# First weights split in the third stage, down weights asked for ahead of the next unit's operands, stores in pieces, low parts of sums apart

## The reference

```python
x = x + 0.5 * quantised_linear(layernorm(x))      # 6-bit weights, unpacked: (w - zero_point) * scale, plus bias
x = x + s4_convolution(layernorm(x))              # causal, 512 long, kernel from a state space model
x = x + 0.5 * quantised_linear(layernorm(x))
x = x + 0.5 * gated_ffn(layernorm(x))             # (silu(x Wg^T) * (x Wu^T)) Wd^T, F = 1376
x = x + s4_convolution(layernorm(x))              # the second state space model
x = x + 0.5 * gated_ffn(layernorm(x))
```

## Time and profile before

| | |
|---|---|
| median of 3 runs | 897.93 us (897.38 to 899.24) |
| profiled execution: its own time | 898.32 us |
| its span, first to last instruction | 896.5 us |
| mean granted TensorE clock | 0.994 |
| PE busy | 880.9 us (98%) |
| DVE busy | 621.2 us (69%) |
| ACT busy | 313.7 us (35%) |
| POOL busy | 372.2 us (42%) |

### The profile page before, as it was taken

How to read it: one execution, slowest core, us unless ns; L and a number is a source line. 1 busy time by engine, 2 the same in 40 slices (tenths; PEclk the granted TensorE clock), 3 DMA queues, 4 the chain that set the end, 5 groups by cost and what they waited for, 6 DMA issues and landing times.

```text
span 896.5 us, 11735 instructions
## 1 busy us (share of the span) xinstructions
PE 880.9 (98%) x4116; PEld 722.2 (81%) x4116; DVE 621.2 (69%) x1058; ACT 313.7 (35%) x517; POOL 372.2 (42%) x728
## 2 busy tenths in 40 slices
PE   8999999999999999999999999999999999999998
PEld 4878887788888877888888878888888788888876
DVE  7989778899999786555566877555667865454553
ACT  4534456534444351222323532222234511122211
POOL 6768567444444343332334452322334532222211
PEclk7999999999999999999999999999999999999999
DMA  8200000166677775564555655464646667556455
GB/s 326 105 1 1 1 1 2 72 240 244 251 272 280 246 232 176 163 183 151 168 163 153 200 165 188 134 189 125 206 142 212 184 179 244 171 180 208 129 158 171
DMA packets 41358, 148.27 MB, mean 165 GB/s; under 512 B 3538, under 2 KB 3794, under 8 KB 39892
## 3 DMA queue, kind: packets, MB, share of 16 engines
q0 software_dynamic: 29040, 100.93, 37.0%
q1 hardware_dynamic: 12260, 46.59, 13.5%
HBM read 117.36 MB, written 30.15 MB: 165 GB/s over the span
## 4 chain that ended last, share of the span: by engine, by line
PE 83%; DVE 6%; POOL 4%; DMA 3%; issue 3%; ACT 2%; SPq 0%; POOLq 0%; ACTq 0%; DVEq 0%
PE front L1469 15%; PE front L1471 15%; PE front L1470 15%; PE acc L1423 8%; PE acc L1425 7%; PE acc L1424 7%; PE front L480 3%; PE acc L1351 3%; PE acc L1350 3%; PE acc L1349 3%; DMA down_weights<-saved_down 2%; DVE hidden_lo L1250 2%; PE front L1351 1%; PE front L1350 1%; PE front L1349 1%
## 5 line engine op out<-in xcount | busy, mean ns | idle before, releaser
L1469 PE MATMUL front<-row_operands_hi,weight_operands 128*128 128x512 f32 x616 | 242.3, 393 | 1.6 <-DVE weight_operands L615 1.5
L1471 PE MATMUL front<-row_operands_hi,weight_operands 128*128 128x512 f32 x616 | 239.9, 390 | 0.0
L1470 PE MATMUL front<-row_operands_lo,weight_operands 128*128 128x512 f32 x616 | 239.9, 389 | 0.0
L1210 DVE TENSOR_TENSOR snapshots<-front,snapshots 128x512 f32<-128x512 f32 x132 | 91.0, 689 | 78.8 <-PE front L1471 77.5
L1423 PE MATMUL acc<-down_weights,hidden_hi 128*128 128x512 f32 x352 | 140.1, 398 | 5.2 <-DMA down_weights<-saved_down 3.4
L1469 PEld LDWEIGHTS front<-row_operands_hi,weight_operands 128*128 128x128 f32 x616 | 115.7, 188 | 28.0 <-issue 2.9
L1425 PE MATMUL acc<-down_weights,hidden_lo 128*128 128x512 f32 x352 | 137.4, 390 | 0.0
L1424 PE MATMUL acc<-down_weights,hidden_hi 128*128 128x512 f32 x352 | 137.2, 390 | 0.0
L1471 PEld LDWEIGHTS front<-row_operands_hi,weight_operands 128*128 128x128 f32 x616 | 115.6, 188 | 24.3
L1470 PEld LDWEIGHTS front<-row_operands_lo,weight_operands 128*128 128x128 f32 x616 | 115.7, 188 | 23.3
L831 POOL DMA_DIRECT2D weight_operands<-saved_weights x66 | 48.6, 736 | 188.4 <-PE front L1471 173.2
(11 more groups left out here) (177 smaller groups left out, 1352.4 us busy)
## 6 DMA issues: line engine op xcount, KB each, us to landing
weight_operands<-saved_weights POOLq DMA_DIRECT2D x33, 1280.0 KB, 6.3
down_weights<-saved_down POOLq DMA_DIRECT2D x77, 512.0 KB, 4.2
saved_weights<-weight_operands SPq DMA_DIRECT2D x11, 1792.0 KB, 6.7
weight_operands<-saved_weights POOLq DMA_DIRECT2D x33, 512.0 KB, 4.2
raw_weights<-wgu SPq DMA_DIRECT2D x11, 512.0 KB, 3.4
saved_down<-down_weights SPq DMA_DIRECT2D x11, 512.0 KB, 3.3
x_rows<-x_in SPq DMA_DIRECT2D x3, 1024.0 KB, 12.1
raw_down<-wdown SPq DMA_DIRECT2D x11, 256.0 KB, 2.9
```

Of the source, the lines that this page charges most:

```text
L1210: V.tensor_tensor(out, sum_of(k, product)[:], other, ALU.add).then_inc(front_read, 1)
L1469: T.matmul(o, wh, xh, start=(j == 0), stop=False)
L1470: T.matmul(o, wh, xl, start=False, stop=False)
L1471: last = T.matmul(o, wl, xh, start=False, stop=(j == 1))
```

## The change

It has four parts; the arithmetic is the same.

1. The split of the weights of step 0 moves from the last items before the units (items 50 to 53) to items 28 to 31 (`WEIGHTS_AT` = 28), on ACT, DVE and POOL.
2. In the last step of a unit POOL asks for the down weights of pass 1 of the turn (`load_down(q + 2)`) before the first operands of the next unit's step 1, and not after them. The wait for the end of the pass now stands ahead of both.
3. The 1024 KB store of the first half is cut into four of 256 KB, each after a further odd pass of the turn (1, 3, 5, 7).
4. In the turns of units 0 to 2, at `j` = 1 to 8, POOL made two low parts after asking for the down weights. Now it waits for the pass, makes one low part, asks for the down weights, and makes the other.

```diff
--- before.py
+++ after.py
@@ -30,6 +30,8 @@
 LN_SLOTS = 8
 
 SECOND_AT = TILES + 2
+
+WEIGHTS_AT = SECOND_AT + 10
 XT_SLOTS = 4
 EMB_SLOTS = 2
 
@@ -701,10 +703,12 @@
                     if u == 3 and f in (2, 4, 6, 8):
                         store(2, 1, f // 2 - 1, f // 2)
                 if u >= 2:
-                    store(u, 0, 0, BLK)
+                    for r in range(BLK):
+                        wait_pass(sp, PASSES * u + FT + 2 * r + 1)
+                        store(u, 0, r, r + 1)
             for r in range(BLK):
                 store(3, 1, r, r + 1)
-            sp.wait_ge(stored, 16 * (2 + 2 * BLK))
+            sp.wait_ge(stored, 16 * 4 * BLK)
 
 
         @block.gpsimd
@@ -815,7 +819,7 @@
                 for later, which in ((3, (0, 1)), (2, (2, 3))):
                     if n + later < PRE and second_of_pair(n + later):
                         sums_lo_step(pool, ITEMS[n + later].number // 2, which)
-                if n == PRE - 3:
+                if n == WEIGHTS_AT + 3:
                     down_weight_lo(pool, 0)
 
             def load_split(k, operands, product, arrived):
@@ -861,9 +865,12 @@
                         rstd_step(pool, n)
                     if q + 1 < FT:
                         down_weight_lo(pool, q + 1)
+
+                    if q + 2 >= FT and f == FT - 1:
+                        load_down(q + 2)
                     if k + 2 >= FT:
                         load_split(k + 2, FIRST_OPERANDS, M7, w_first_in)
-                    if q + 2 >= FT:
+                    if q + 2 >= FT and f < FT - 1:
                         load_down(q + 2)
                     if k + 2 >= FT:
                         load_split(k + 2, LAST_OPERANDS, M3, w_last_in)
@@ -875,9 +882,15 @@
                 for n in STATS_OF_STEP[u][FT - 1]:
                     rstd_step(pool, n)
                 for j in range(-1, FT - 1):
-                    load_down(PASSES * u + FT + j + WD_RING)
+
                     if u + 1 < UNITS and 1 <= j <= 2 * BLK:
-                        sums_lo_step(pool, BLK * (u + 1) + (j - 1) // 2, (0, 1) if j % 2 else (2, 3))
+                        pair, first = BLK * (u + 1) + (j - 1) // 2, 0 if j % 2 else 2
+                        wait_pass(pool, PASSES * u + FT + j)
+                        sums_lo_step(pool, pair, (first,))
+                        load_down(PASSES * u + FT + j + WD_RING)
+                        sums_lo_step(pool, pair, (first + 1,))
+                    else:
+                        load_down(PASSES * u + FT + j + WD_RING)
 
 
         @block.scalar
@@ -937,9 +950,9 @@
                     den_square()
                 if n in (13, SECOND_AT + 6):
                     toe_round(0 if n == 13 else 1)
-                if n == PRE - 6:
+                if n == WEIGHTS_AT:
                     weight_hi_raw(act, 0)
-                if n == PRE - 4:
+                if n == WEIGHTS_AT + 2:
                     weight_hi_sums(act, 0)
                     down_weight_hi(act, 0)
 
@@ -1196,11 +1209,11 @@
                     strip_lo(0 if n == 14 else 1)
                 if n in (13, SECOND_AT + 6):
                     strip(0 if n == 13 else 1)
-                if n == PRE - 6:
+                if n == WEIGHTS_AT:
                     weight_sums_a(dve, 0)
-                if n == PRE - 5:
+                if n == WEIGHTS_AT + 1:
                     weight_sums_b(dve, 0)
-                if n == PRE - 3:
+                if n == WEIGHTS_AT + 3:
                     weight_lows(dve, 0, (RAW, SUMS, FOURTH))
 
             def add(k, product, read, out, other):
```

## The result

The changed kernel takes 892.71 us, the median of 4 runs (891.92 to 893.25). The kernel before, beside it, takes 897.91 us (897.38 to 899.24). The ratio on record is 0.9935, with a 95% interval of 0.9923 to 0.9947. The profiled execution took 892.72 us, with a span of 890.9 us.

What follows compares the result with a forecast made beforehand. PE, busy 880.9 of 896.5 us, was taken as the bound, so only its waits count. Terms -1.0 - 1.0 + 0.35 - 1.4 - 0.4 - 1.1 = -4.6 us gave 893.3 us, range 891.8 to 896.3.

Steps and rivals of the forecast that it cites:

- What bounds the kernel: Whole span: PE is busy 880.9 of 896.5 us, so only its waits, 6.5 us at the places named, can be won.
- Part 1: Start of unit 0: PE's 1.48 us wait for the first low parts goes, less 0.5 of lateness: -1.0 us.
- the lateness of 0.5 us at the first pair: Third stage: DVE reaches the first pair's sums 0.2 to 1.3 us late, taken as 0.5, all passed on to PE.
- Part 2: Turns of units 0 and 1: -1.0 us (1.34 wait gone, new 0.3 before pass 2), then a loss of 0.35.
- Unit 2: Turn of unit 2: the 1.64 us wait before pass 2 shrinks to 0.2, a gain of 1.4 us.
- Part 3 in unit 3: Unit 3: loads beside a 256 KB piece land in 4.8 us, within about 5.0, so the 0.40 wait goes: -0.4 us.
- Part 4: Turns of units 0 to 2: six waits for `hidden_lo` go, 1.37 us, less 0.25 for later loads: -1.1 us.
- the 0.25 set aside for late loads: Turns of units 0 to 2: cost of down-weight loads issued 0.75 us later, set at 0.25 us in all (0 to 1.0).
- the third stage takes it back: Rival, chance 0.17: DVE 1.5 us late at the first pair, late loads eat half the `hidden_lo` gain; -3.1, 894.8 us.
- parts 2 and 3 don't do what they say: Rival, chance 0.11: queued transfers share engines, unit 0's wait stays, unit 1 gets 1.0, unit 2 keeps half; -2.35, 895.6 us.
- an issue stands behind DVE: Rival, chance 0.05: in the turns POOL's issue waits for DVE's `hidden_lo`, each load 0.4 us later; -2.2, 895.7 us.
- The slow series: Rival, chance 0.04: the four transfers at each turn land 13 us after first issue, not 10.1; +4.4, 902.3 us.

Runs made afterwards that it cites:

- run 8: The changed kernel with DVE's three low parts of the first weights one item later, behind the first pair's sums: 894.70 us, ratio 0.9961.
- run 3: The changed kernel with the operands again asked for before the down weights at every turn: 892.10 us, ratio 0.9912.
- run 12: The kernel before with only the first-half stores cut into 256 KB pieces, measured again for a profile: 896.72 us, ratio 0.9983.
- run 1: The kernel before with only the split of the first weights moved to earlier items: 897.21 us, ratio 0.9973.
- run 2: The kernel before with only POOL's two low parts set apart, the down-weight load between them: 896.24 us, ratio 0.9965.
- run 4: The changed kernel with one 1024 KB first-half store per unit again instead of four pieces: 899.48 us, ratio 1.0000.
- run 10: The changed kernel with down weights ahead of the operands in the turn of unit 0 alone, unit 3's store still in pieces: 892.81 us, ratio 0.9923.
- run 5: The changed kernel with down weights ahead in unit 0 alone and unit 3's first-half store as one transfer behind the ninth pass: 890.52 us, ratio 0.9907.
- run 6: The changed kernel with only unit 3's first-half store made one 1024 KB transfer behind the ninth pass: 892.84 us, ratio 0.9934.
- run 11: The changed kernel with down weights ahead in unit 0 alone and unit 3's store whole behind the ninth pass, measured again: 890.89 us, ratio 0.9916.
- run 9: The changed kernel as it is, measured again against the kernel before: 892.79 us, ratio 0.9933.

## Why the forecast was right, and where it was not

**What bounds the kernel**, and that only PE's waits can be won, holds: every microsecond of the gain lies at one of the places that the earlier trace rows led to.

**Part 1** was forecast at -1.0 and is -1.8. The step that failed is the lateness of 0.5 us at the first pair, with its lower end of 0.2: measured is 0. It took DVE's listed idle time, 1.92 us, as the whole cover, where 2.04 or a little more were there for 2.05 of work, and had POOL's bias meet the end of the low parts. POOL's operations were the ones to stand, its bias moved away, and the pair began on time. The other 0.3 us are the hidden price of the wait. That the chain has no cover for lateness is right (run 8).

**Part 2** in units 0 and 1 is right in place and sign, each within 0.25 us: no wait before pass 1, a new one of 0.35 before pass 2, a loss at unit 1. Terms of the same size with opposite signs cancel, so that the part is worth nothing beside the others (run 3).

**Unit 2** is right for the sum of parts 2 and 3 (-1.2 for -1.4). What the forecast did not price is what either would do alone. Part 3 alone brings -1.9 at this wait (run 12), more than the two together. Part 2 without it costs some 5 us: parts 1 and 4 alone gain 1.8 and 2.8 us (runs 1 and 2), and run 4, which has both and part 2, gains nothing.

**Part 3 in unit 3** has the wrong sign: +0.49 for -0.4. The step that failed is the landing of "4.2 + 0.6 = 4.8 us" for a load beside a piece. As a mean it is near: 22 such loads, in the six profiles with pieces in unit 3, land after 4.9 us. But they spread from 3.9 to 7.1, and one that takes more than the 5.1 to 5.2 us that are there is enough. In the profile of the change it takes 5.9. The wait of 0.40 did go, and a larger one came at 879 us. Waits of 0.19 to 1.56 us stand there in four of the six profiles (the change, runs 3, 10 and 12) and in none of the three in which the store comes late (runs 5, 6 and 11), whose loads take 3.6 to 4.0 us. In two more with pieces (runs 8 and 9) no load was slow enough. So the pieces make the wait possible, and chance decides each time whether it comes; why one load takes 4 and the next 6 us stays open.

**Part 4** has the right mechanism and is mis-sized: -3.15 for -1.1. The term that was mis-sized is what a removed wait is worth: the forecast took the listed 0.2 us, and some 0.5 came. Of the 2.0 missing, some 1.6 are the 0.27 us at each of six waits beyond their listed idle time; the rest is the 0.25 set aside for late loads, and rounding. That the profiled execution did not pay for late loads was luck: in six of ten profiles with part 4 they cost 0.35 to 1.2 us at the place near 336 us (run 9). The load was issued 0.5 us later than before, not 0.75.

**The sum** is 1.1 us short for the profiled executions (-4.6 for -5.7) and 0.6 us for the medians. It is so near since the two gains that were too small, 2.9 us together, stand against a start-up 0.39 later, 0.9 lost in unit 3 and 0.5 in the turns. That the forecast was nearer than its terms is luck.

**The rivals.** That the third stage takes it back, and that parts 2 and 3 don't do what they say, is ruled out by the steps; the down weights in front land 3.9 us after their issue in unit 0. The first of the two has a slip in its sum: 1.0 and 0.5 us lost are 1.5, without the -1.0 in front, and 894.8 us stands. That an issue stands behind DVE is ruled out by the landings. The slow series is real: the fourth transfer lands 9.7 to 10.5 us after the first issue in 16 of the 18 series of this order, after 12.9 in one (run 8) and after 13.7 with the whole store inside (run 4).

## What to carry to other kernels

A wait of the bound engine is worth more than its listed idle time; match the instructions of two traces and read the difference of start times, which prices each place, chance ones too. When a transfer is moved in front of another, add up everything that shares the engines until the last one that is needed, and look when each can be issued: the same move won 1.2 us at one turn, lost 0.6 and 0.8 at two others, and with a store in the middle cost the whole gain. Give a load that shares with a store the spread of its landings, not their mean. And a median over few runs can hide a real step of 1 us behind a load that is late by chance or a fall of the clock; the trace at the place tells them apart.

## What the runs showed of the hardware

A wait of PE costs beyond its idle time: the successor of the first matmul after it starts 0.31 to 0.34 us later instead of 0.23, in the rows shown here at the full clock.

A wait of PE for a load of 3.40 us ends in a granted clock of 0.50, that is 1.2 instead of 2.4 GHz, from 698.5 to 705.3 us, with matmuls 0.43 us apart (run 8). Behind the 4.20 us of run 4 the granted clock is 0.61 from 698.7 to 702.5 us. TensorE: Matmul & The Clock Gate of the Trainium skill ("HAM oscillation — how this bites in real kernels") has such a fall of the clock behind a wait for a DMA; the two traces agree. None of the waits for down weights of up to 1.64 us did it, so the longest waits cost more than their length: 1.6 us more in run 4, 2.8 in run 8.

The clock also fell without a long wait. In runs 2, 3, 10 and 12 it is at 0.50 for 3.4 us that begin at 50 to 52 us. Ahead of it PE had been busy since its wait of 0.7 us before 48 to 49 us, with sixteen matmuls of 16 columns among wide ones. The row is of run 2, the granted clock behind POOL's number:

```profile
52.00:56.00 4.00, 4.00 (x13) 3.08 (x13) 2.95 (x13) 0.00 (x0) 2.12 (x4) 0.57 0.00 0
```

The same work stands there in the nine other profiles whose clock was recorded, and theirs did not fall. It costs 1.6 us each time. Why it comes in some executions stays open.

A small store beside loads is not always small: the same 256 KB take 2.0 to 6.0 us in the change, in unit 3 alone 2.02, 3.06, 5.99 and 5.84, and a load issued beside the 5.99 takes 5.90.

The series of four transfers, 2816 KB, has landed 9.7 to 10.5 us after its first issue in 16 of 18 cases and after 12.9 in one without a store in its first 9 us. What made that one slow stays open: between 694.0 and 699.2 us the engines moved 290 GB/s.
